# Merging two accumulators at the end of an expert stage: VectorE adds and plain stores in place of GpSimd scatters

## The chip, the cores and the metric

The kernel runs on one core of one Trainium2 chip. The metric is the device time of one execution in microseconds (us); the median of three runs stands for a kernel. A profile is one more execution, taken with the hardware profiler. It has its own time, and a span from its first to its last instruction.

## The reference, cut to what matters

A small vision-tower layer: a state-space kernel makes the tokens, a class token is added, then come attention and a mixture of 32 experts with the best 4 for each token, plus one shared expert. The end of it is what the change touches:

```python
probs = zeros((T, 32)).at[arange(T)[:, None], idx].set(topv)      # T = 2056 tokens, 4 experts each
for (wg, wu, wd, p) in experts:                                   # 32 of them
    acc = acc + p[:, None] * (silu(clip(x @ wg.T)) * clip(x @ wu.T)) @ wd.T
out = h + acc + shared_expert(x)                                  # (2056, 512) f32
```

## The kernel before, in words

Tokens are handled in 17 tiles of 128 rows by 512 columns of f32 (`NT = 17`; the last tile has 8 real rows, the rest of it is scratch). One tile is 256 KB, all 17 are 4.46 MB. The program runs four stages one after the other: `ssm_stage`, `attention_stage`, `route_stage`, `expert_stage`. Each is a block in which all engines run their own instruction streams and meet at its end.

`route_stage` leaves in DRAM the normalised tokens (`x_rows`), the output `acc` (named `out_dram` in the profile) holding the residual plus the shared expert (stores at L968), and a second accumulator `acc2` (`acc_rows` in the profile) filled with zeros (17 stores from a zero tile, L960).

`expert_stage` goes over slots. A slot is up to 128 tokens of one expert; there are 96 slots in 24 passes of four (`UN = 4`), and a pass whose slots are all empty is skipped by a value that each engine reads (`used`, L1401). In this input 21 passes are used and the last three are skipped. In a slot GpSimd gathers the rows (L1562), TensorE transposes them and multiplies with the expert's weights (L1468, L1505), which SP loads (L1419), ScalarE scales the result into `ys` (L1527), and GpSimd scatters `ys` into an accumulator with an add done by the DMA (L1594): even slots into `acc`, odd slots into `acc2`. So two neighbouring slots never add into the same tensor at once. SP waits for each scatter to land (L1441) and passes that on by `landed` and `sent`.

After the passes comes the merge, which is what the change rewrites:

- SP leaves its loop over the passes, then reads the number of used passes four times (`turns`, L1405) and waits each time for the last weight loads (L1444), and only then issues 17 loads of 256 KB from `acc2` into the SBUF tile `back` (L1448).
- GpSimd waits until the first six tiles of `back` are in (then the next six, then the last five, `PARTS`) and issues 17 indirect scatters, one for a tile, that add `back` into `acc` by row numbers held in `rowids` (L1617). `rowids` is a small table loaded by SP at the start of the stage (L1412), between the load of `ident` (L1411) and the first weights (L1416 to L1419).
- GpSimd waits until all 17 have landed. The program ends there.

TensorE, VectorE and ScalarE have no work in the merge.

Of the kernel before, what the change touches and what calls it, by code (L numbers as in the profile page):

```python
# [11 lines left out]
DM = 512  # L12
# [5 lines left out]
NT = 17  # L18
# [5 lines left out]
UN = 4  # L24
# [1319 lines left out]
def expert_stage(nc, T, slot_info, slot_rows):  # L1344
# [6 lines left out]
    f32, i32 = mybir.dt.float32, mybir.dt.uint32  # L1351
    ALU, ACT = mybir.AluOpType, mybir.ActivationFunctionType
# [6 lines left out]
    with ExitStack() as ctx:  # L1359
        sb = lambda name, shape, dt=f32: ctx.enter_context(nc.sbuf_tensor("ex_" + name, shape, dt))  # L1360
        sem = lambda name: ctx.enter_context(nc.semaphore("ex_" + name))
        rowids = sb("rowids", [128, NT], i32)
        back = sb("back", [128, NT, DM])
        rowids_ready, added, landed = sem("rowids_ready"), sem("added"), sem("landed")
        PARTS = [range(0, 6), range(6, 12), range(12, NT)]
        rows_back = [sem(f"rows_back{k}") for k in range(len(PARTS))]
        ident = sb("ident", [128, 128])
        wt = sb("wt", [128, WBUF * WCOLS])
        gidx = [sb(f"gidx{n}", [128, 1], i32) for n in range(4)]
# [24 lines left out]
        pe_turn, pool_turn, sp_turn = (sem(n) for n in ("pe_turn", "pool_turn", "sp_turn"))  # L1394
# [4 lines left out]
        def used(engine, it):  # L1399

            return engine.If(engine.value_load(slot_info[0:1, bass.ds(it * (4 * UN) + 3, 1)], min_val=0, max_val=1))  # L1401

        def turns(engine):

            return engine.value_load(slot_info[0:1, 4 * 127 + 3:4 * 128], min_val=1, max_val=ITERS)  # L1405

        with nc.Block() as block:

            @block.sync
            def _(sp):  # L1410
                sp.dma_start(ident[:], T["ident"]).then_inc(ident_ready, 16)  # L1411
                sp.dma_start(rowids[:], T["rowids"]).then_inc(rowids_ready, 16)  # L1412

                def load(slot, n):

                    expert = sp.value_load(slot_info[0:1, bass.ds(slot * 4, 1)], min_val=0, max_val=NEXP - 1)  # L1416
                    first = sp.value_load(slot_info[0:1, bass.ds(slot * 4 + 1, 1)], min_val=0, max_val=1)
                    buf = sp.value_load(slot_info[0:1, bass.ds(slot * 4 + 2, 1)], min_val=0, max_val=WBUF - 1)
                    sp.dma_start(wt[:, bass.ds(buf * WCOLS, WCOLS)],  # L1419
                                 T["wexp"][bass.ds(expert, 1), :, :].rearrange("o p n -> p (o n)"),  # L1420
                                 cond=first).then_inc(w_ready[n % UN], 16)

                for slot in range(AHEAD):
                    if slot >= UN:
                        sp.wait_ge(w_ready[slot % UN], 16)
                        sp.sem_inc(sp_turn, 1)
                    load(slot, slot)
                sp.sem_inc(y_full, W_SEED)
                sp.sem_inc(landed, 2)
                with sp.Fori(0, ITERS) as it:  # L1430
                    with used(sp, it):
                        for n in range(UN):

                            sp.wait_ge(y_full, it * UN + n - 2 + W_SEED)
                            sp.sem_inc(sp_turn, 1)
                            sp.wait_ge(w_ready[(n + AHEAD) % UN], (it + (n + AHEAD) // UN - 1) * 16 + 16)
                            sp.sem_inc(sp_turn, 1)
                            load(it * UN + n + AHEAD, n + AHEAD)

                            sp.wait_ge(scattered[n % 2], (it * (UN // 2) + n // 2) * 16 + 16)  # L1440
                            sp.sem_inc(landed, 1)  # L1441
                            sp.sem_inc(sent, 1)
                for n in range(UN):
                    sp.wait_ge(w_ready[n], turns(sp) * 16 + (32 if n < AHEAD - UN else 16))  # L1444
                    sp.sem_inc(sp_turn, 1)
                for k, part in enumerate(PARTS):
                    for t in part:
                        sp.dma_start(back[:, t, :], T["acc2"][128 * t:128 * t + 128, :]).then_inc(rows_back[k], 16)  # L1448

            @block.tensor  # L1450
            def _(pe):
# [58 lines left out]
            @block.scalar  # L1510
            def _(act):
                A = nc.scalar
                act.sem_inc(ta_taken, TA_SEED)
                act.sem_inc(y_ready, Y_SEED)
                act.sem_inc(sent, SENT_SEED)
                with act.Fori(0, ITERS) as it:
                    with used(act, it):
                        for n in range(UN):
                            s = it * UN + n
                            act.wait_ge(gate_ready, s + 1)  # L1520
                            A.activation(sil[:], gc[:], ACT.Silu).then_inc(silu_ready, 1)  # L1521
                            act.wait_ge(ta_full, s + 1)
                            A.copy(actT[:].rearrange("p c t -> p (c t)"), ta[:, 0:FF]).then_inc(ta_taken, 1)
                            act.wait_ge(y_full, s + 1 + W_SEED)
                            act.wait_ge(sent, s + 1)
                            act.wait_ge(share_ready, s + 1)
                            A.activation(ys[n][:], yb[n % 2][:], ACT.Copy, scale=share[:, n:n + 1]).then_inc(y_ready, 1)  # L1527

            @block.vector
            def _(dve):  # L1530
                V = nc.vector

                def take_rows(n, count):
                    dve.wait_ge(tx_full, count)
                    V.tensor_copy(xT[n % 2][:].rearrange("p k t -> p (k t)"), tx[:]).then_inc(tx_taken, 1)  # L1535

                dve.sem_inc(tx_taken, TX_SEED)
                dve.sem_inc(gu_taken, GU_SEED)
                take_rows(0, 1)
                take_rows(1, 2)  # L1540
                with dve.Fori(0, ITERS) as it:  # L1541
                    with used(dve, it):
                        for n in range(UN):
                            s = it * UN + n
                            dve.wait_ge(gu_full, s + 1)
                            V.tensor_scalar(gc[:], gu[n % 2][:, 0:FF], -ALPHA, ALPHA, ALU.max, ALU.min).then_inc(gate_ready, 1)  # L1546
                            V.tensor_scalar(uc[:], gu[n % 2][:, FF:2 * FF], -ALPHA, ALPHA, ALU.max, ALU.min).then_inc(gu_taken, 1)  # L1547
                            dve.wait_ge(gu_taken, s + 2)
                            dve.wait_ge(silu_ready, s + 1)
                            V.tensor_tensor(act_[:], sil[:], uc[:], ALU.mult).then_inc(act_ready, 1)  # L1550
                            take_rows(n + 2, s + 3)

            @block.gpsimd
            def _(pool):
                P = nc.gpsimd
# [29 lines left out]
                with pool.Fori(0, ITERS) as it:  # L1585
                    with used(pool, it):
                        for n in range(UN):
# [8 lines left out]
                                                 None, compute_op=ALU.add).then_inc(scattered[n % 2], 16)  # L1596
# [9 lines left out]
                last = turns(pool)  # L1606
                for n in range(4):

                    pool.wait_ge(gathered[n], last * 16 + (32 if n < 2 else 16))
                    pool.sem_inc(pool_turn, 1)  # L1610
                pool.wait_ge(landed, last * UN + 2)
                pool.sem_inc(pool_turn, 1)
                pool.wait_ge(rowids_ready, 16)
                for k, part in enumerate(PARTS):
                    pool.wait_ge(rows_back[k], 16 * len(part))
                    for t in part:
                        P.indirect_dma_start(T["acc"], bass.IndirectOffsetOnAxis(ap=rowids[:, t:t + 1], axis=0), back[:, t, :],  # L1617
                                             None, compute_op=ALU.add).then_inc(added, 16)
                pool.wait_ge(added, 16 * NT)


def build(nc, T):
# [16 lines left out]
def laid_out(x, cls_tok, L0_tok_log_dt, L0_tok_B_ri, L0_tok_inv_A_real, L0_tok_A_imag, L0_attn_c_attn_w, L0_attn_c_attn_b,  # L1639
# [9 lines left out]
    k, v = slice(DM, DM + HD), slice(DM + HD, DM + 2 * HD)  # L1649
    selh = np.zeros((128, 4, 128), np.float32)  # L1650
    for j in range(4):
# [6 lines left out]
    row, col = np.arange(128)[:, None], np.arange(128)[None, :]  # L1658
# [14 lines left out]
        "upper": (row < col).astype(np.float32),  # L1673
        "iota": np.broadcast_to(col, (128, 128)).astype(np.float32),
        "rowid": row.astype(np.float32),
        "rowids": (row + 128 * np.arange(NT)[None, :]).astype(np.uint32),
        "isrow": (row < NCH).astype(np.float32),
        "router": chunks(L0_ffn_router_w.T),
        "ebias": L0_ffn_expert_bias.reshape(1, NEXP),
# [18 lines left out]
```

## Time and profile before

| | |
|---|---|
| median of 3 runs | 1371.49 us (1370.15 to 1372.88) |
| time of the profiled execution | 1373.46 us |
| its span | 1371.7 us |
| granted TensorE clock, mean | 0.916 of full speed |
| TensorE busy | 1059.8 us (77%) |
| VectorE, ScalarE, GpSimd busy | 633.5, 360.5, 427.0 us |
| moved by DMA | 138.05 MB |

The span is 1.76 us shorter than the profiled execution's own time, and that time is 1.97 us over the median of the runs. Differences worked out in the span are therefore applied to the median. A busy share is an average over four stages with different limits; the merge is the last 50 us or so and is read by itself. In the profile a name such as SPq or POOLq is an engine's sequencer: instructions that issue, read a register or wait. The DMA share of a stretch is the mean busy share of the core's 16 DMA engines, and it can read slightly over 1.

### The profile page before, as it was taken

How to read it: one execution, taken by the hardware profiler on the slowest of the kernel's cores; microseconds unless marked ns; L12 is line 12 of the kernel's file. 1: busy time of each engine (PE TensorE's matmuls, PEld its weight loads, DVE VectorE, ACT ScalarE, POOL GpSimd, SP SyncE). 2: the span in 40 equal slices, each digit the busy share in tenths (PEclk: the TensorE clock that was granted, in tenths of full speed). 3: DMA queues.
4: the chain of work that ended last, by engine and by line, in shares of the span. 5: the costliest groups of instructions: out<-in, count | busy, mean ns of one | idle time of the engine just before them, and what ended most of it. 6: DMA issues, size and time to landing. Idle time of an engine off the chain costs nothing. (4 is left out here: it accounts for less than half of the span.)

```text
span 1371.7 us, 23002 instructions
## 1 busy us (share of the span) xinstructions
PE 1059.8 (77%) x5647; PEld 648.9 (47%) x5649; DVE 633.5 (46%) x1459; ACT 360.5 (26%) x1030; POOL 427.0 (31%) x602
## 2 busy tenths in 40 slices
PE   0444368888868888859898399999999999999910
PEld 0343367677657777734344144444444444444400
DVE  8999744543426544563986523233232332323300
ACT  2111035454425554513100012222222222222200
POOL 0000032122012221110007634545545455454535
PEclk9766779999979999979999699999999999999965
DMA  4144400000000000041051348666687877656868
GB/s 151 25 69 77 77 1 2 1 1 2 1 3 1 1 1 1 2 141 60 1 193 46 105 103 227 134 183 175 182 227 178 254 197 195 169 132 168 240 170 130
DMA packets 58684, 138.05 MB, mean 101 GB/s; under 512 B 22624, under 2 KB 23648, under 8 KB 53872
## 3 DMA queue, kind: packets, MB, share of 16 engines
q0 software_dynamic: 21744, 51.56, 20.1%
q1 hardware_dynamic: 36864, 85.55, 18.6%
q8 instruction: 39, 0.64, 0.2%
q14 instruction: 37, 0.30, 0.1%
HBM read 180.81 MB, written 44.35 MB: 164 GB/s over the span
## 5 line engine op out<-in xcount | busy, mean ns | idle before, releaser
L1468 PE MATMUL ex_gu<-ex_wt,ex_xT 128*128 x680 | 324.7, 600 | 16.3 <-DVE ex_uc L1547 9.2
L1468 PEld LDWEIGHTS ex_gu<-ex_wt,ex_xT 128*128 128x128 f32 x680 | 121.9, 192 | 146.9 <-issue 146.9
L1535 DVE COPY ex_xT<-ex_tx 128x512 f32<-128x512 f32 x86 | 59.5, 691 | 252.0 <-PE ex_tx L1459 252.0
L1505 PE MATMUL ex_y<-ex_wt,ex_actT 128*128 x336 | 158.1, 593 | 0.0
L1527 ACT ACTIVATE ex_ys<-ex_y,ex_share 128x512 f32<-128x512 f32 x84 | 57.7, 687 | 294.3 <-PE ex_y L1505 287.3
L639 ACT ACTIVATE at_pg<-at_S,at_nmax 128x129 f32<-128x129 f32 (+1 forms) x256 | 104.9, 423 | 72.0 <-DVE at_nmax L751 65.3
L751 DVE TENSOR_REDUCE at_nmax<-at_S 128x1 f32<-128x129 f32 (+1 forms) x256 | 81.9, 353 | 78.2 <-PE at_S L519 72.6
L1562 POOL DMA_INDIRECT ex_xg<-x_rows,ex_gidx x90 | 90.3, 1004 | 73.4 <-POOL ex_gidx L1559 71.3
L1594 POOL DMA_INDIRECT out_dram<-ex_ys,ex_sidx x42 | 67.1, 1597 | 97.0 <-ACT ex_ys L1527 96.2
L329 PE MATMUL ssm_ps<-ssm_v,ssm_q 64*64 64x64 f32 x1024 | 46.6, 273 | 63.5 <-DVEq L287 63.5
L1594 POOL DMA_INDIRECT acc_rows<-ex_ys,ex_sidx x42 | 66.9, 1593 | 82.8 <-ACT ex_ys L1527 77.1
L1550 DVE TENSOR_TENSOR ex_act<-ex_sil,ex_uc 128x256 f32<-128x256 f32 x84 | 35.8, 426 | 115.5 <-ACT ex_sil L1521 115.5
L817 POOL TENSOR_TENSOR at_rstd<-at_ve,at_power 128x2 f32<-128x2 f32 x8 | 5.7, 712 | 245.2 <-DVE at_ve L687 245.2
L1340 POOL TENSOR_SCALAR rt_rowsel<-rt_iota,rt_posf 128x128 bf16<-128x128 f32 x68 | 45.6, 689 | 106.1 <-DVE rt_posf L1279 99.1
L329 PEld LDWEIGHTS ssm_ps<-ssm_v,ssm_q 64*64 64x64 f32 x1024 | 45.5, 183 | 65.3 <-DVEq L287 65.3
L1505 PEld LDWEIGHTS ex_y<-ex_wt,ex_actT 128*128 128x128 f32 x336 | 57.3, 190 | 40.2 <-issue 40.2
L1023 PE MATMUL rt_p<-rt_xT,rt_sgu 128*128 128x512 f32 (+1 forms) x160 | 64.9, 571 | 5.1 <-DVE rt_uc L1163 4.6
L1459 PEld LDWEIGHTS ex_tx<-ex_ident,ex_xg 128*128 128x128 f32 x344 | 43.2, 142 | 53.8 <-issue 53.8
L1567 POOL COPY ex_share<-ex_xg 128x1 f32 x86 | 65.8, 765 | 1.4 <-DMA ex_xg<-x_rows,ex_gidx 1.4
L1570 POOL COPY ex_sidx<-slot_rows 128x1 uint32 (+1 forms) x85 | 64.8, 762 | 0.0
L1459 PE MATMUL ex_tx<-ex_ident,ex_xg 128*128 128x128 f32 x344 | 52.1, 274 | 8.4 <-DMA ex_xg<-x_rows,ex_gidx 8.4
L519 PE MATMUL at_S<-at_maskb,at_identb 128*128 128x128 bf16 x256 | 57.7, 225 | 0.0
(305 smaller groups left out, 2020.9 us busy)
## 6 DMA issues: line engine op xcount, KB each, us to landing
ex_wt<-in_wexp_dram SPq DMA_DIRECT2D x89, 1536.0 KB
acc_rows<-rt_zero SPq DMA_DIRECT2D x17, 256.0 KB, 5.2
x_rows<-rt_xa SPq DMA_DIRECT2D x16, 272.0 KB
ex_back<-acc_rows SPq DMA_DIRECT2D x17, 256.0 KB, 5.7
ssm_rows<-ssm_c SPq DMA_DIRECT2D x8, 512.0 KB, 3.8
H<-ssm_rows SPq DMA_DIRECT2D x16, 256.0 KB, 5.6
out_dram<-H SPq DMA_DIRECT2D x16, 256.0 KB
at_watt<-in_watt_dram SPq DMA_DIRECT2D x1, 1536.0 KB, 8.5
```

The lines of the kernel that those rows point to most:

```text
L329: last = nc.tensor.matmul(ps[n][h, i, :], qb[n][h, r, i].rearrange("q c a -> q (c a)"), vb[n][h, r, i, :], start=(r == 0), stop=(r == 1))
L639: A.activation(pg[:, g % 2, m, 0:keys], S[m][:, 0:keys], ACT.Exp, bias=nmax[:, m:m + 1], accum_out=r2[:, n % 2, 4 * j + m:4 * j + m + 1]). ...
L751: V.tensor_reduce(out=nmax[:, m:m + 1], in_=S[m][:, 0:keys], axis=AX.X, op=ALU.max, negate=True).then_inc(max_done, 1)
L1023: last = M(gu[m][:, 0:n], sgu[:, kc, 128 * m:128 * m + 128], xT[:, kc, 128 * tiles[0]:128 * tiles[0] + n], start=(kc == 0), stop=(kc == KC ...
L1459: last = nc.tensor.transpose(tx[:, 128 * kc:128 * kc + 128], xg[n % 4][:, 128 * kc:128 * kc + 128], ident[:])
L1468: last = M(gu[n % 2][:], xT[n % 2][:, kc, :], wt[:, bass.ds(base + kc * 2 * FF, 2 * FF)], start=(kc == 0), stop=(kc == KC - 1))
L1505: last = M(yb[n % 2][:], actT[:, c, :], wt[:, bass.ds(base + KC * 2 * FF + c * DM, DM)], start=(c == 0), stop=(c == FC - 1))
L1535: V.tensor_copy(xT[n % 2][:].rearrange("p k t -> p (k t)"), tx[:]).then_inc(tx_taken, 1)
L1562: P.indirect_dma_start(xg[n % 4][:], None, T["x2"], bass.IndirectOffsetOnAxis(ap=gidx[n % 4][:], axis=0)).then_inc(gathered[n % 4], 16)
L1567: P.tensor_copy(share[:, n % 4:n % 4 + 1], xg[n % 4][:, bass.ds(expert + DM, 1)]).then_inc(share_ready, 1)
L1570: P.tensor_copy(sidx[n % UN][:], slot_rows[:, bass.ds(slot, 1)]).then_inc(sidx_ready, 1)
L1594: P.indirect_dma_start(T["acc2"] if n % 2 else T["acc"], bass.IndirectOffsetOnAxis(ap=sidx[n][:], axis=0), ys[n][:], None, compute_op=ALU. ...
```

## The change

Both accumulators are loaded into SBUF: `acc2` into `odd` by SP, `acc` into `even` by ScalarE's queue. Each is loaded in five parts of 4, 4, 4, 3 and 2 tiles, one DMA for a part. VectorE adds a part as soon as both of its halves are in, and SP stores it to `acc`. `rowids`, its load and the 17 scatters are gone. The waits for the last weight loads with their reads of `turns` now come after the stores have been issued, and SP waits for the stores at the end. ScalarE starts its loads when SP signals that it has left its loop (`all_landed`).

```diff
--- before.py
+++ after.py
@@ -1359,11 +1359,11 @@
     with ExitStack() as ctx:
         sb = lambda name, shape, dt=f32: ctx.enter_context(nc.sbuf_tensor("ex_" + name, shape, dt))
         sem = lambda name: ctx.enter_context(nc.semaphore("ex_" + name))
-        rowids = sb("rowids", [128, NT], i32)
-        back = sb("back", [128, NT, DM])
-        rowids_ready, added, landed = sem("rowids_ready"), sem("added"), sem("landed")
-        PARTS = [range(0, 6), range(6, 12), range(12, NT)]
-        rows_back = [sem(f"rows_back{k}") for k in range(len(PARTS))]
+        odd, even = sb("odd", [128, NT, DM]), sb("even", [128, NT, DM])
+        landed, all_landed, summed, stored = sem("landed"), sem("all_landed"), sem("summed"), sem("stored")
+        PARTS = [range(0, 4), range(4, 8), range(8, 12), range(12, 15), range(15, NT)]
+        odd_back = [sem(f"odd_back{k}") for k in range(len(PARTS))]
+        even_back = [sem(f"even_back{k}") for k in range(len(PARTS))]
         ident = sb("ident", [128, 128])
         wt = sb("wt", [128, WBUF * WCOLS])
         gidx = [sb(f"gidx{n}", [128, 1], i32) for n in range(4)]
@@ -1409,7 +1409,6 @@
             @block.sync
             def _(sp):
                 sp.dma_start(ident[:], T["ident"]).then_inc(ident_ready, 16)
-                sp.dma_start(rowids[:], T["rowids"]).then_inc(rowids_ready, 16)
 
                 def load(slot, n):
 
@@ -1440,12 +1439,18 @@
                             sp.wait_ge(scattered[n % 2], (it * (UN // 2) + n // 2) * 16 + 16)
                             sp.sem_inc(landed, 1)
                             sp.sem_inc(sent, 1)
+                sp.sem_inc(all_landed, 1)
+                for k, part in enumerate(PARTS):
+                    rows = T["acc2"][128 * part[0]:128 * part[-1] + 128, :].rearrange("(t p) d -> p t d", p=128)
+                    sp.dma_start(odd[:, part[0]:part[-1] + 1, :], rows).then_inc(odd_back[k], 16)
+                for k, part in enumerate(PARTS):
+                    rows = T["acc"][128 * part[0]:128 * part[-1] + 128, :].rearrange("(t p) d -> p t d", p=128)
+                    sp.wait_ge(summed, k + 1)
+                    sp.dma_start(rows, odd[:, part[0]:part[-1] + 1, :]).then_inc(stored, 16)
                 for n in range(UN):
                     sp.wait_ge(w_ready[n], turns(sp) * 16 + (32 if n < AHEAD - UN else 16))
                     sp.sem_inc(sp_turn, 1)
-                for k, part in enumerate(PARTS):
-                    for t in part:
-                        sp.dma_start(back[:, t, :], T["acc2"][128 * t:128 * t + 128, :]).then_inc(rows_back[k], 16)
+                sp.wait_ge(stored, 16 * len(PARTS))
 
             @block.tensor
             def _(pe):
@@ -1525,6 +1530,10 @@
                             act.wait_ge(sent, s + 1)
                             act.wait_ge(share_ready, s + 1)
                             A.activation(ys[n][:], yb[n % 2][:], ACT.Copy, scale=share[:, n:n + 1]).then_inc(y_ready, 1)
+                act.wait_ge(all_landed, 1)
+                for k, part in enumerate(PARTS):
+                    rows = T["acc"][128 * part[0]:128 * part[-1] + 128, :].rearrange("(t p) d -> p t d", p=128)
+                    act.dma_start(even[:, part[0]:part[-1] + 1, :], rows).then_inc(even_back[k], 16)
 
             @block.vector
             def _(dve):
@@ -1549,6 +1558,11 @@
                             dve.wait_ge(silu_ready, s + 1)
                             V.tensor_tensor(act_[:], sil[:], uc[:], ALU.mult).then_inc(act_ready, 1)
                             take_rows(n + 2, s + 3)
+                for k, part in enumerate(PARTS):
+                    tiles = slice(part[0], part[-1] + 1)
+                    dve.wait_ge(odd_back[k], 16)
+                    dve.wait_ge(even_back[k], 16)
+                    V.tensor_tensor(odd[:, tiles, :], odd[:, tiles, :], even[:, tiles, :], ALU.add).then_inc(summed, 1)
 
             @block.gpsimd
             def _(pool):
@@ -1608,15 +1622,6 @@
 
                     pool.wait_ge(gathered[n], last * 16 + (32 if n < 2 else 16))
                     pool.sem_inc(pool_turn, 1)
-                pool.wait_ge(landed, last * UN + 2)
-                pool.sem_inc(pool_turn, 1)
-                pool.wait_ge(rowids_ready, 16)
-                for k, part in enumerate(PARTS):
-                    pool.wait_ge(rows_back[k], 16 * len(part))
-                    for t in part:
-                        P.indirect_dma_start(T["acc"], bass.IndirectOffsetOnAxis(ap=rowids[:, t:t + 1], axis=0), back[:, t, :],
-                                             None, compute_op=ALU.add).then_inc(added, 16)
-                pool.wait_ge(added, 16 * NT)
 
 
 def build(nc, T):
@@ -1673,7 +1678,6 @@
         "upper": (row < col).astype(np.float32),
         "iota": np.broadcast_to(col, (128, 128)).astype(np.float32),
         "rowid": row.astype(np.float32),
-        "rowids": (row + 128 * np.arange(NT)[None, :]).astype(np.uint32),
         "isrow": (row < NCH).astype(np.float32),
         "router": chunks(L0_ffn_router_w.T),
         "ebias": L0_ffn_expert_bias.reshape(1, NEXP),
```

## Rows read from the trace of the kernel before

**Rows 1.** Chain of waits, expert stage only: shares by line.

```profile
by line: PE ex_gu L1468 57.6%; PE ex_y L1505 21.1%; PE ex_tx L1459 7.2%; PE ex_ta L1497 5.7%; issue 3.4%; DVEq L1401 2.2%; DVE ex_uc L1547 1.6%; DVEq L1541 0.6%; DVE ex_gc L1546 0.4%; DVE ex_xT L1535 0.3%; DVEq L1545 0.2%
```

**Rows 2.** Chain of waits, last slot to first scatter of the merge: start, length, what.

```profile
1309.30 0.69 ACT ex_ys L1527
...
1310.80 4.69 DMA acc_rows<-ex_ys,ex_sidx
...
1315.60 0.06 issue
...
1319.70 0.27 SPq L1405
...
1322.56 0.35 SPq L1448
...
1324.85 4.72 DMA ex_back<-acc_rows
...
1330.39 1.60 POOL out_dram L1617
```

**Rows 3.** Chain of waits, its last piece.

```profile
1360.18 1.55 POOL out_dram L1617
```

**Rows 4.** Busy time by stretch: five engines' busy us, TensorE's clock, DMA share, GB/s.

```profile
1322.56:1323.60 1.04, 0.00 (x0) 0.00 (x0) 0.00 (x0) 0.00 (x0) 0.00 (x0) 0.50 0.09 14
1324.00:1330.00 6.00, 0.00 (x0) 0.00 (x0) 0.00 (x0) 0.00 (x0) 0.00 (x0) 0.50 0.93 319
1326.00:1327.00 1.00, 0.00 (x0) 0.00 (x0) 0.00 (x0) 0.00 (x0) 0.00 (x0) 0.50 0.72 260
1340.00:1360.00 20.00, 0.00 (x0) 0.00 (x0) 0.00 (x0) 0.00 (x0) 16.82 (x11) 0.50 1.06 154
1364.00:1365.00 1.00, 0.00 (x0) 0.00 (x0) 0.00 (x0) 0.00 (x0) 0.00 (x0) 0.50 0.74 129
1365.00:1366.00 1.00, 0.00 (x0) 0.00 (x0) 0.00 (x0) 0.00 (x0) 0.00 (x0) 0.50 0.11 18
```

**Rows 5.** DMA queues, 1322 to 1372 us: packets, MB, share of 16 engines' time.

```profile
q0 software_dynamic: 2448, 4.46, 59.4%
q1 hardware_dynamic: 2448, 4.46, 25.9%
```

**Rows 6.** Start of the expert stage, chain of waits.

```profile
775.32 0.42 SPq L1412
...
775.77 0.51 SPq L1416
...
778.12 7.89 DMA ex_wt<-in_wexp_dram
...
787.11 6.59 PE ex_gu L1468 x8
```

**Rows 7.** Busy time by stretch, three others with the DMA engines full.

```profile
610.00:622.00 12.00, 10.36 (x44) 6.34 (x45) 11.52 (x30) 4.87 (x9) 3.17 (x2) 0.77 1.05 404
5.00:12.00 7.00, 0.00 (x0) 0.00 (x0) 6.45 (x20) 0.00 (x0) 0.00 (x0) 1.00 1.01 417
708.00:712.00 4.00, 3.85 (x9) 1.62 (x10) 3.86 (x6) 0.00 (x0) 0.00 (x0) 1.00 1.01 374
```

**Rows 8.** SP's DMA issues by line: ns min/median/max, first and last start.

```profile
L960 SPq DMA_DIRECT2D acc_rows<-rt_zero x17: 432/655/1411, 605.3 to 618.2; - x17
L137 SPq DMA_DIRECT2D ssm_rows<-ssm_c x8: 376/377/393, 61.9 to 161.4; - x8
```

**Rows 9.** VectorE groups by form: count, busy us, mean ns, idle.

```profile
L244 DVE TENSOR_TENSOR ssm_products<-ssm_c,ssm_work 128x2048 f32<-128x2048 f32 x2 | 4.5, 2284 | 0.0
L246 DVE TENSOR_TENSOR ssm_q_low<-ssm_products 128x1024 f32<-128x1024 f32 x1 | 1.2, 1224 | 0.0
```

**Rows 10.** Line L1617, issue to landing of its 17 scatters.

```profile
DMA to landing us min/median/max: 4.9/5.6/8.0
```

**Rows 11.** Busy time by stretch, one load of 16 partitions (L133).

```profile
68.00:69.00 1.00, 0.00 (x0) 0.00 (x0) 1.00 (x2) 0.00 (x0) 0.00 (x0) 0.50 1.06 107
```

## Prediction, on record before the changed kernel was run

> **What bounds the kernel now.** I began with the chain of waits over the expert stage. Four TensorE lines hold 91.6% of it [rows 1], so until 1309.30 the kernel goes at TensorE's pace, and nothing that VectorE, ScalarE or GpSimd do in the passes matters. Then I read the chain through the end [rows 2]. The last scatter of the passes is issued at 1310.80 and lands 4.69 us later. SP then walks through three skipped passes, and by 1319.70 it has left its loop. From 1319.70 to 1322.56 it only reads `turns` four times. Then it issues the loads of `acc2`. The first six tiles are in at 1329.57, GpSimd begins at 1330.39, and its last scatter is issued from 1360.18 for 1.55 us [rows 3]. The 17 scatters take (1361.73 - 1330.39) / 17 = 1.84 us each.
>
> The view of busy time by stretch says what else is full there. Between 1340 and 1360 GpSimd is busy for 16.82 of 20 us, but the DMA engines show a share of 1.06 while they move only 154 GB/s [rows 4]. So the merge is bound twice: by GpSimd's issue and by adding transfers that occupy the DMA engines far longer than plain ones. The view of the queues puts a price on that. 17 plain loads and 17 adding scatters move the same 4.46 MB, the loads for 25.9% and the scatters for 59.4% of the 16 engines' 50 us [rows 5]. That is 12.95 us against 29.7 us. TensorE, VectorE and ScalarE are idle there. DMA activity ends at about 1365.15 (share 0.74 in 1364 to 1365, 0.11 in the next us [rows 4]); to the end of the span at 1371.7 there are 6.55 us of landing and of the program's end.
>
> From SP's first load at 1322.56 to the end of DMA activity the merge so takes 42.6 us.
>
> **The change part by part.**
>
> The four reads of `turns` move behind the stores. SP can issue its first load where the reads begin now: 1322.56 - 1319.70 = 2.86 us sooner [rows 2], less about 0.05 us for the new signal to ScalarE. Gain **2.8 us**. The moved reads and their waits for weights, long landed, stand behind the last store's issue on SP. Nobody waits for them but SP's own last wait, and the stores in flight cover them; without that cover they would cost their 2.86 us again.
>
> The load of `rowids` goes. SP issues it from 775.32, and the weights' first instruction follows at 775.77; the weights set when the first multiplication starts [rows 6]. So everything behind moves by **0.45 us**. The chain from there on is TensorE's [rows 1], and I take the gain as kept; the other end is 0.
>
> The issue of the new DMAs. Ten large ones take the place of 17 loads on SP; each holds 512 pieces of 2 KB (384 or 256 in the last two). SP issues a DMA of 2,048 pieces in 0.38 us, no more than one of 128 pieces [rows 2, 8], so issue isn't a term. ScalarE's issue isn't in this trace; by the nearest row it is 0.4 us, and as both queues feed the same full engines, even 1 us there would be hidden behind the `odd` part that SP has already issued. Where the engines can't keep up, the issuing sequencer is held: for the 17 zero stores the median is 0.655 us, 256 KB / 0.655 us = 400 GB/s, the transfer's pace [rows 8]. SP will be held so in its loads, and the stores issued after them start later; but ScalarE and SP have nothing else to do, and the engines are full meanwhile.
>
> The traffic is the big term. 2 x 4.46 MB are loaded and 4.46 MB stored. Loads: the nearest row is the present load of `acc2`, the same tensor, rows and direction. It took 12.95 us of all engines [rows 5], or 344 GB/s; twice that is 25.9 us. The ends: the 319 GB/s of its undisturbed stretch [rows 4] gives 8.92 MB / 319 = 27.9 us, the 417 GB/s of the program's first loads [rows 7] gives 21.4 us. I take 25.9. Stores: the zero stores have the same form and ran at 404 GB/s [rows 7], 11.0 us; the slower end is the 374 GB/s of the stores at 708 to 712 us, 11.9 us. Together 36.9 us. Engines take 1.04 us after the first issue to begin, with a share of 0.09 until then [rows 4]: I use 1.1 us. From the first issue to the end of activity the new merge takes 38.0 us in place of 42.6. Gain **4.6 us**.
>
> A rule speaks for more. The Trainium skill, page "DMA: Bandwidth & Descriptors", section "Bandwidth", asks for transfers of 1 MiB and more, and its table has 425 GB/s for 16 MB against 138 for 64 KB. By that the loads would take 21.0 us, and the whole gain would be 4.9 us larger. The rows don't bear it out as a rule of size: the zero stores reached 404 GB/s with 256 KB each [rows 7, 8].
>
> VectorE's additions. A part of four tiles is 128x2048, 2.28 us [rows 9]; two tiles 1.22; three about 1.75 between them: 3 x 2.28 + 1.75 + 1.22 = 9.8 us. They lie under 36.9 us of traffic. The last counts only if the engines run dry before its store arrives. Behind the last load there are about 1.5 us of landing (estimate from the 1.04 us of start), the 1.22 us addition, 0.43 us of issue and 1.1 us of start: 4.2 us. Covering it are the stores of the parts before, 15 tiles or 3.93 MB, 9.7 us at 404 GB/s, if they are still due then. I take 0; uncovered it is 4.2 us.
>
> The end. GpSimd's scatters land 4.9 to 8.0 us after issue, median 5.6 [rows 10], so most of the 6.55 us is the program's end, which stays. I take no change; 1 us less, as GpSimd then reaches its end early, or 1.5 us more are the ends.
>
> The sum: 2.8 + 0.45 + 4.6 = **7.85 us**. The profiled span is 1371.7 us (its execution 1373.46, 1.97 over the median of 1371.49); the difference goes on the median: 1371.49 - 7.85 = **1363.6 us**.
>
> **The rivals.**
>
> *The loads run as fast as the engines can.* 417 GB/s for the loads saves 4.5 us more, and 1 us goes at the end: 1358.1 us. For it: two queues and larger DMAs keep more pieces waiting at every engine, and the share fell to 0.72 in one microsecond of the present load [rows 4]. Against it: that load was issued faster (256 KB in 0.47 us) than it moved, so a lack of issued work wasn't its limit.
>
> *The engines run dry before the last store.* If stores pass in among the loads, little is left when the last load lands, and 4.2 us show: 1367.8 us. For it: stores and loads share the engines, and the first part is summed long before the last has landed. Against it: SP's stores are issued behind all of its loads, and SP is held in those.
>
> *The rows of a part are read in an order that the memory or the engines serve badly, and it gets slower.* Now each DMA moves 256 KB that lie together. The new ones take for each partition four rows that lie 256 KB apart. This has one place, the 13.37 MB of the merge, and one price. The gains leave 42.6 - 1.1 + 2.8 + 0.45 = 44.75 us for them, so it is slower than now below 13.37 MB / 44.75 = 299 GB/s, and by over 0.2% below 281. At the 260 GB/s of the present load's worst microsecond [rows 4] it takes 51.4 us: 1371.49 + 6.7 = 1378.2 us. The far row is the load of `H`, whose rows too go several to a partition, with 107 GB/s at a share of 1.06 [rows 11]: 125 us, some 1452 us. But that one fills 16 partitions, the new ones 128 like the present loads. A rule stands beside it: the same page of the Trainium skill, section "Latency and other measured facts", has copies falling to 207 GB/s when the rows of neighbouring partitions lie 512 KiB apart. By it the merge would take 65 us and the kernel about 1392. Here neighbouring partitions lie 2 KB apart and only the four rows of one partition are far apart, and no run so far shows such a load.
>
> **How the numbers follow.** This kernel's runs lie within 0.2% of each other, 2.7 us, so less than that can't be told from no change. The forecast case has a chance of 0.54, its own range 1360 to 1368.5 (loads at 319, stores at 374 GB/s and a longer end give 39.8 us of traffic and 3.0 us of gain). Fast loads have 0.20, the dry engines 0.12, the badly served rows 0.14. For 8 in 10 I go from 1357 to 1370: it holds nearly all of the first three. Faster by over 0.2% (under 1368.8): 0.53 + 0.20 + 0.09 = 0.82. Slower (over 1374.2): 0.10 of the badly served rows. The same: what is left, 0.08.
>
> **What would show it.** SP's first load at about 1319.3, the chain's first multiplication 0.45 us sooner. Over the merge a DMA share near 1 and 340 to 400 GB/s without a gap. DMA activity ending near 1357, and 6.5 us after it. Five additions of 2.28, 1.75 and 1.22 us, the first at about 1327. The prediction is wrong if the loads' rate lies under 300 GB/s, if a stretch of low share stands between the last load and the last store, or if the end grows by several us.

## The result, and the profile after

Timed on one chip with the kernel before, the changed kernel took 1355.12 us (median of 4, 1354.44 to 1357.51) against 1372.18. The ratio is 0.9879, 95% interval 0.9861 to 0.9898: 17.1 us faster, between 14.0 and 19.1. Forecast were 1363.6 us and a range from 1357 to 1370; the direction was right, the gain was about twice the forecast, and the time lies below the range. Timed again later, the same kernel took 1354.69 us.

The profiled execution took 1354.81 us, its span is 1352.8. First the chain of waits at the end of the passes, to be read against [rows 2]:

```profile
1305.14 0.69 ACT ex_ys L1532
...
1306.64 4.44 DMA acc_rows<-ex_ys,ex_sidx
...
1311.69 0.26 SPq L1401
...
1312.99 0.27 SPq L1401
...
1314.26 0.26 SPq L1401
...
1315.29 0.51 ACTq L1536
1315.83 0.55 ACTq L1536
...
1321.33 20.90 DMA ex_even<-out_dram
...
1342.33 1.22 DVE ex_odd L1565
```

From the last `ys` to the first load there are 10.15 us, where before there were 13.26 (1309.30 to 1322.56): the reads of `turns` are out of the way. What stays in front is the landing of the last scatter and three skipped passes of 1.28 us each (L1401, from one start to the next).

The view of busy time by stretch over the merge (five engines, TensorE's clock, DMA share, GB/s), against [rows 4]:

```profile
1316.00:1318.00 2.00, 0.00 (x0) 0.00 (x0) 0.00 (x0) 0.00 (x0) 0.00 (x0) 0.50 0.61 102
1318.00:1323.00 5.00, 0.00 (x0) 0.00 (x0) 0.00 (x0) 0.00 (x0) 0.00 (x0) 0.50 0.97 347
1323.00:1342.00 19.00, 0.00 (x0) 0.00 (x0) 8.64 (x4) 0.00 (x0) 0.00 (x0) 0.50 1.04 391
1342.00:1351.00 9.00, 0.00 (x0) 0.00 (x0) 1.22 (x1) 0.00 (x0) 0.00 (x0) 0.50 1.05 409
1351.00:1352.00 1.00, 0.00 (x0) 0.00 (x0) 0.00 (x0) 0.00 (x0) 0.00 (x0) 0.50 0.86 332
```

The engines are full from 1318 to the end of activity at about 1351.9. The first microseconds are slow (347 GB/s), as they were before (319), then come 391 and 409. From the first load to the end of activity there are 36.6 us in place of 42.5. The additions lie under the traffic: the one of two tiles ends at 1343.55, and the engines are busy for 8 us after it.

Then the instructions of line L1407, where the stage's block ends, which the prediction left out. Each row has the engine, the kind, its ns and its start; a drain is the instruction with which an engine closes its part of the block. First the kernel before, then the changed one.

```profile
L1407 POOLq COMPARE_BRANCH  x1: 46/46/46, 1365.9 to 1365.9; - x1
L1407 POOLq DRAIN  x1: 5369/5369/5369, 1366.1 to 1366.1; - x1
```

```profile
L1407 POOLq DRAIN  x1: 3985/3985/3985, 1313.8 to 1313.8; - x1
...
L1407 DVEq DRAIN  x1: 1236/1236/1236, 1342.4 to 1342.4; - x1
L1407 SPq COMPARE_BRANCH  x1: 38/38/38, 1352.4 to 1352.4; - x1
L1407 SPq DRAIN  x1: 13/13/13, 1352.6 to 1352.6; - x1
```

In this stage GpSimd ends with a drain of 4 to 5.4 us. Before, it began at 1366.1, when the last scatter had landed, and ended at 1371.5: it was the end of the program. Now it runs from 1313.8 to 1317.8 beside the loads, and SP, which waits for the stores, drains in 0.013 us. From the end of DMA activity to the end of the span there are 0.9 us in place of 6.6. GpSimd's drain isn't long everywhere. This is the one at the end of the attention stage (L467), in which GpSimd computes but issues no DMA, from the trace of the kernel before:

```profile
L467 POOLq DRAIN  x1: 53/53/53, 555.4 to 555.4; - x1
```

What makes it 0.05 us there and 4 us in the expert stage no run separates; GpSimd's gathers and scatters are one difference between the two.

So the 18.9 us between the two spans are: 4.2 us up to the last `ys`, 3.1 from there to the first load, 5.9 in the traffic, 5.7 at the end.

### The profile page after: what moved, and what is told of

It reads as the page before. It is cut to its first block and busy times, and to the rows that moved or that the text cites. A ratio compares the mean times of both kernels' runs of the same rounds, so it can differ in the third digit from the quotient of the medians.

```text
span 1352.8 us, 22990 instructions
## 1 busy us (share of the span) xinstructions
PE 1057.3 (78%) x5647; PEld 648.3 (48%) x5649; DVE 643.6 (48%) x1464; ACT 360.6 (27%) x1030; POOL 400.9 (30%) x585
## 5 line engine op out<-in xcount | busy, mean ns | idle before, releaser
L1023 PE MATMUL rt_p<-rt_xT,rt_sgu 128*128 128x512 f32 (+1 forms) x160 | 62.1, 550 | 5.1 <-DVE rt_uc L1163 4.6
```

Source lines behind the costliest of these rows:

```text
L1023: last = M(gu[m][:, 0:n], sgu[:, kc, 128 * m:128 * m + 128], xT[:, kc, 128 * tiles[0]:128 * tiles[0] + n], start=(kc == 0), stop=(kc == KC ...
```

## The experiments

Each is read by stage: last `ys` to first load, first load to the end of DMA activity ("traffic"), and that to the end of the span ("end"). The changed kernel has 10.15, 36.6 and 0.9 us; timed again, 10.5, 36.2 and 1.2. The end of activity is read from stretches of 0.25 us, so traffic and end are good to a few tenths of a us. The time up to the last `ys` differs by some microseconds between executions of one program and isn't read from single ones; only in the part on the table it is compared, counted from the start of the stage.

**Whose wait it is.** In the kernel before, SP waits for the scatters in place of GpSimd.

```diff
+                sp.wait_ge(added, 16 * NT)     # SP, after its loads
-                pool.wait_ge(added, 16 * NT)
```

> The kernel before, with one edit: SP, not GpSimd, waits for the 17 scatters to land, so that GpSimd reaches the end of its block right after issuing them. Theory (the drain of GpSimd at the end of the block is a fixed cost that began only after its wait): the drain of about 5.4 us now begins about 4.3 us sooner, beside the landing of the last scatter, so from the end of DMA activity to the end of the span there are 1.5 to 2.5 us in place of 6.55, and the time falls by 4 to 5 us. Rival (adding scatters are reported late, whoever waits for them): the stretch stays at 6 to 6.6 us and the time stays.

1370.67 us against 1372.75 in one execution each; the end is 4.8 us in place of 6.6.

```profile
1359.40 1.55 POOL L1618 DMA_INDIRECT out_dram<-ex_back,ex_rowids  x1 [0.30 <-issue]
```

```profile
L1407 POOLq DRAIN  x1: 29963/29963/29963, 1338.7 to 1338.7; - x1
L1407 SPq COMPARE_BRANCH  x1: 38/38/38, 1365.1 to 1365.1; - x1
L1407 SPq DRAIN  x1: 13/13/13, 1365.3 to 1365.3; - x1
```

SP passes its wait at 1365.1, so the scatters have landed by then. GpSimd's drain stands in its queue from 1338.7, while its scatters are still being issued, the last from 1359.40 for 1.55 us; it ends at 1368.7 (1338.7 + 29.96). That is 3.6 us after the landing. So both expectations missed: the end shrank, by 1.8 us and not by 4 to 5. Freed of the wait, GpSimd still ends the program, and its drain is still running 5.4 us after its last scatter was issued (1360.95).

**GpSimd waits too.** In the changed kernel, GpSimd also waits for the last store.

```diff
+                pool.wait_ge(stored, 16 * len(PARTS))     # GpSimd's last instruction
```

> The changed kernel, with one edit: GpSimd also waits for the last store before it ends. Theory (GpSimd's drain is hidden only because GpSimd ends early): the span's stretch after the last DMA activity grows from 0.9 us to about 5, by the 4.0 us that the drain takes in the changed kernel. Rival (the 6.55 us belonged to the scatters): it stays at about 1 us.

1358.13 us in one execution; traffic 36.2, end 5.2 us.

```profile
L1407 POOLq COMPARE_BRANCH  x1: 43/43/43, 1351.7 to 1351.7; - x1
L1407 POOLq DRAIN  x1: 3987/3987/3987, 1351.9 to 1351.9; - x1
L1407 SPq DRAIN  x1: 13/13/13, 1351.9 to 1351.9; - x1
```

Here no adding scatter is near, everything has landed, and the drain still takes 3.99 us after GpSimd's last wait. With one wait the 4 us are back: the end is 4.3 us longer than in the changed kernel, 4.0 longer than in its repeat. So the drain behind GpSimd's wait is the cause of about 4 of the 5.7 us at the end. The other 1.4, by which the drain of the kernel before was longer (5.37 against 3.99), no run explains.

**GpSimd stores.** In the changed kernel, the five stores are issued by GpSimd; SP waits for them.

```diff
-                    sp.wait_ge(summed, k + 1)
-                    sp.dma_start(rows, odd[:, part[0]:part[-1] + 1, :]).then_inc(stored, 16)
+                    pool.wait_ge(summed, k + 1)     # the loop moves to GpSimd's end
+                    P.dma_start(rows, odd[:, part[0]:part[-1] + 1, :]).then_inc(stored, 16)
```

> The changed kernel, with the five plain stores issued by GpSimd instead of SP; SP still waits for them and GpSimd only issues. The last store lands some 9 us after its issue, since the stores before it are queued. Theory (GpSimd's drain can't be done before what GpSimd has issued has landed, and takes 3.6 to 5.4 us after that): from the end of DMA activity to the end of the span there are 4.5 to 6.5 us. Rival (the drain is a fixed piece of 4 to 8 us after GpSimd's last instruction): it is over when the last store lands, and the stretch stays at 1 to 1.5 us.

1357.07 us in one execution; traffic 36.6, end 4.2 us, which is outside both expectations. The premise was wrong: on GpSimd's queue the stores pass in among the loads, so that the last one landed 3.2 us after its issue and not 9, and the last loads came later instead.

```profile
1346.97 1.22 DVE L1561 TENSOR_TENSOR ex_odd<-ex_odd,ex_even 128x1024 f32<-128x1024 f32 x1 [1.73 <-DMA ex_even<-out_dram]
1348.49 0.71 POOL L1624 DMA_DIRECT2D out_dram<-ex_odd  x1 [2.21 <-DVE ex_odd L1561]
```

The view of that store alone, and then line L1407:

```profile
DMA to landing us min/median/max: 3.2/3.2/3.2
```

```profile
L1407 POOLq DRAIN  x1: 6233/6233/6233, 1348.5 to 1348.5; - x1
L1407 SPq COMPARE_BRANCH  x1: 38/38/38, 1351.7 to 1351.7; - x1
```

The drain ends at 1354.7, 3.0 us after SP sees the landing, and again it is the end of the program. In the kernel before and these three it ended 3.0 to 5.6 us after the last landing. That it waits for what GpSimd issued fits the first and third experiments, but as no transfer here landed long after its issue, it isn't separated from a drain that simply ends 5.5 to 7.8 us after the last issue.

**The reads of `turns` in front again.** In the changed kernel they move from behind the stores to their old place:

```diff
+                for n in range(UN):
+                    sp.wait_ge(w_ready[n], turns(sp) * 16 + (32 if n < AHEAD - UN else 16))
+                    sp.sem_inc(sp_turn, 1)
                 sp.sem_inc(all_landed, 1)
```

> The changed kernel, with the reads of the number of passes and their waits for weights back in front of the loads. Theory: SP's first load of the merge issues 2.8 to 2.9 us later after the last scatter's landing, and the whole merge behind it is unchanged, so plus 2.8 us. Rival (the reads were hidden, since ScalarE or the engines weren't ready before): less than 1 us.

Last `ys` to first load: 13.16 us, 3.0 more; traffic 36.3, end 1.1; 1358.56 us in one execution. The term stands.

```profile
1305.89 0.70 ACT ex_ys L1532
...
1316.16 0.27 SPq L1405
...
1319.05 0.50 ACTq L1536
```

**One queue; small loads; rows together.** Three edits of the traffic in the changed kernel: all loads on SP; 17 loads of 256 KB on each queue; and the rows dealt to the partitions in another way.

```diff
-                    act.dma_start(even[:, part[0]:part[-1] + 1, :], rows).then_inc(even_back[k], 16)
+                    sp.dma_start(even[:, part[0]:part[-1] + 1, :], rows).then_inc(even_back[k], 16)     # first edit
...
+                    for t in part:                                                                      # second edit
+                        sp.dma_start(odd[:, t, :], T["acc2"][128 * t:128 * t + 128, :]).then_inc(odd_back[k], 16)
...
-  .rearrange("(t p) d -> p t d", p=128)
+  .rearrange("(p t) d -> p t d", p=128)                                # third edit, loads and stores
```

> The changed kernel, with both accumulators loaded by SP, part by part in turn, and none by ScalarE. Theory (the 16 engines were full either way, and my 344 GB/s was low because the profile's share of the old loads counts time in which adding scatters shared the engines): the merge from SP's first load to the end of DMA activity stays at 36.5 us, within 1 us, with about 385 GB/s once it has started. Rival (two queues are what keeps the engines full): about 340 to 350 GB/s for the loads, 39 to 40 us.

> The changed kernel, with 17 loads of 256 KB on each of the two queues in place of five large ones; the stores stay large. Theory (size doesn't matter once the engines are full): the merge stays at 36.5 us, within 1 us. Rival (large transfers are what brought the rate): the loads go at 320 to 350 GB/s, and the merge takes 38.5 to 40 us.

> The changed kernel, with the rows of a part dealt so that the four, three or two rows of a partition lie together in DRAM, 8 KB in one piece, for the loads and the stores alike; the sum is the same. Theory (rows 256 KB apart cost nothing here): the merge stays at 36 to 36.6 us. Rival (the far rows do cost): the rate rises from 390 towards the 417 GB/s of the program's first loads, which have pieces of 8 and 12 KB, and the merge takes 33 to 34.5 us.

Traffic: 36.3, 35.4 and 33.7 us; single executions of 1357.68, 1357.24 and 1355.30 us. The view of stretches, for one queue, then for small loads, then for rows together:

```profile
1320.00:1325.00 5.00, 0.00 (x0) 0.00 (x0) 0.00 (x0) 0.00 (x0) 0.00 (x0) 0.50 0.93 333
1325.00:1345.00 20.00, 0.00 (x0) 0.00 (x0) 9.16 (x5) 0.00 (x0) 0.00 (x0) 0.50 1.05 391
```

```profile
1320.00:1325.00 5.00, 0.00 (x0) 0.00 (x0) 0.00 (x0) 0.00 (x0) 0.00 (x0) 0.50 1.01 368
1325.00:1345.00 20.00, 0.00 (x0) 0.00 (x0) 8.84 (x5) 0.00 (x0) 0.00 (x0) 0.50 1.05 391
```

```profile
1324.00:1347.00 23.00, 0.00 (x0) 0.00 (x0) 9.86 (x5) 0.00 (x0) 0.00 (x0) 0.50 1.01 415
```

Neither the second queue nor the size of a transfer brought the rate: 391 GB/s each time once it runs, after a slower start. So the rivals of the first two are out, though the small loads fell just outside the 36.5 us within 1 that the theory gave them. For the third, the theory is out: rows that lie together, up to 8 KB in a piece, move at 415 GB/s, and the traffic takes 2.5 to 2.9 us less than with rows that lie 256 KB apart (36.2 and 36.6 us in two executions of the changed kernel). The small loads, which read 256 KB that lie together in pieces of 2 KB, gain 0.8 to 1.2 us; so how much of the gain is the distance and how much the piece isn't settled.

**The even accumulator earlier.** ScalarE doesn't wait for SP's signal but for the last scatter into `acc`.

```diff
-                act.wait_ge(all_landed, 1)
+                act.wait_ge(scattered[0], turns(act) * (16 * UN // 2))
```

> The changed kernel, with ScalarE itself waiting for the last scatter into the even accumulator, by the number of passes, instead of for SP's signal; SP still loads the odd one after its loop. Theory (the merge is bound by its traffic from the first load on, and SP's three skipped passes of 1.28 us each stand in front of it): ScalarE's first load issues 4.5 to 5 us sooner, the engines are busy from then on, and the time falls by 4 to 5 us against the changed kernel, to about 1350.5 us. Rival (SP's late odd loads set the end): less than 1.5 us.

1352.25 us, 0.9858 (0.9842 to 0.9875) of the kernel before, 2.9 us under the changed kernel's median of 1355.12 and short of the 4 to 5 expected. ScalarE's first load comes 3.80 us after the last `ys` in place of 10.15, but the traffic takes 38.1 us: until 1316 the engines move 252 GB/s, while the last scatter and the last gathers still run beside it.

```profile
1305.91 0.69 ACT L1531 ACTIVATE ex_ys<-ex_y,ex_share 128x512 f32<-128x512 f32 x1 [3.50 <-PE ex_y L1509]
...
1309.71 6.56 ACTq L1535 DMA_DIRECT2D ex_even<-out_dram  x5
```

```profile
1309.50:1316.00 6.50, 0.00 (x0) 0.00 (x0) 0.00 (x0) 0.00 (x0) 1.12 (x2) 0.50 0.97 252
```

From the last `ys` to the end of activity the profiled execution is 4.8 us shorter than the changed kernel's; of these 0.4 are lost at the end, and its last `ys` came 0.8 later, which the edit doesn't touch.

**The table of row numbers.** Its load is put back in the changed kernel, though nothing reads it (SP only waits for it at its very end); run once, then in rounds beside the changed kernel.

```diff
                 sp.dma_start(ident[:], T["ident"]).then_inc(ident_ready, 16)
+                sp.dma_start(rowids[:], T["rowids"]).then_inc(rowids_ready, 16)
```

> The changed kernel, with the load of the table of row numbers put back at its old place, though nothing reads it. Theory (only its issue was on the path): SP's first weight load issues 0.45 us later in its stage, and the first weights land about 6.5 us after issue as in the changed kernel; everything else as there. Rival (the table's 128 small pieces or the shifted addresses of all later tiles slow the first weights and the loads of the merge): the first weights take 7.5 to 8 us and the loads of the merge run below 350 GB/s.

> The changed kernel with the load of the table of row numbers put back, timed in rounds, since its single execution was 6 us over the changed kernel's median, most of it in the passes. Theory (the table costs its issue of 0.45 us and no more; the passes vary by some us between executions): the median is within 1.5 us of the changed kernel timed beside it. Rival (the shifted tiles or the small pieces slow the passes): 4 to 6 us above it.

> The changed kernel itself, timed again beside the others. Every theory: 1354 to 1357 us, 0.986 to 0.990 of the kernel before.

The single execution took 1360.93 us, the four in rounds 1357.07 (0.9889, 0.9874 to 0.9905); the changed kernel beside them 1354.69 (0.9876, 0.9858 to 0.9894). The merge is the same in both (traffic 36.4 and 36.5 us), so shifted tiles don't slow it. The medians are 2.4 us apart, more than the theory's 1.5 and less than the rival's 4; the intervals overlap. The single execution was no measure: 1.5 of its 6 us came before the stage began, and its first `ys` and its last lie 510.8 us apart, against 507.6 to 508.2 in the other three executions with the table. One place where the table could cost is the first weights, in the chain of waits of the table's execution in rounds:

```profile
775.88 7.85 DMA ex_wt<-in_wexp_dram
```

With the table they took 7.5 to 7.9 us in all four profiled executions that have it (the kernel before is one of them), without it 6.5 to 9.0 with a median of 6.65 in ten. So the rival of the single run was right about the first weights and wrong about the merge.

The last `ys` came between 1306.7 and 1311.0 in the four, between 1304.4 and 1308.1 in the ten. But the stage itself began at 772.7 to 777.1, by what happened before it. Counted from its first instruction, SP's load of `ident`, the passes can be compared in single executions. Here is that start in the kernel before, to be read with [rows 6]:

```profile
774.92 0.35 SPq L1411
```

And in the changed kernel:

```profile
773.97 0.36 SPq L1411
...
776.71 6.47 DMA ex_wt<-in_wexp_dram
...
784.28 5.18 PE ex_gu L1473 x8
```

The first multiplication starts 12.19 us into the stage before (774.92 to 787.11) and 10.31 after. From the start of the stage to the last `ys` there are 532.8 to 535.6 us in the four with the table (median 534.2; 534.1 without the single execution) and 530.7 to 533.7 in the ten without it (median 531.1). Only one of the ten is in the range of the four, the one whose first weights took 9.0 us. So by the traces the table was worth about 3 us. 0.45 of them are its issue, and about 1 the later landing of the first weights; where the rest lies no run shows.

**Both improvements.** The early wait and the rows together.

> ScalarE's own early wait together with the rows of a part dealt so that they lie together. Theory (the two gains are in different terms, the start of the traffic and its rate): from ScalarE's first load to the end of DMA activity 35 to 36 us in place of 38.1, and a time of 1349 to 1350.5 us, 0.983 to 0.985 of the kernel before. Rival (SP's odd loads come too late for the faster engines): no faster than with the early wait alone, 1352 us.

1347.01 us (1345.81 to 1348.52), 0.9816 (0.9802 to 0.9829) of the kernel before: 25 us faster than it and 7.7 under the changed kernel's median beside it. Traffic 36.2 us from a first load 3.78 us after the last `ys`.

```profile
1308.90:1315.00 6.10, 0.00 (x0) 0.00 (x0) 0.00 (x0) 0.00 (x0) 1.00 (x1) 0.50 0.89 264
1315.00:1340.00 25.00, 0.00 (x0) 0.00 (x0) 9.75 (x5) 0.00 (x0) 0.00 (x0) 0.50 1.01 417
```

Behind the mixed start the engines run at 417 GB/s. From the last `ys` to the end of the span the profiled executions took 47.7 us in the changed kernel and 48.0 in its repeat, 43.3 with the early wait, 45.5 with the rows together and 41.5 with both. So the gains nearly add up, as is to be expected when one starts the traffic sooner and the other raises its rate. The traffic missed its 35 to 36 us by a little, and the time came out below the expected 1349. Of the 7.7 us in the medians the merge has 6.2 to 6.5; the rest no run explains.

## Why the prediction was half right

*The reads of `turns`, 2.8 us.* Right: 3.0 to 3.1.

*The end, "I take no change".* This is the step that failed. I had read that a scatter lands 5.6 us after its issue and that 6.55 us follow the end of DMA activity, and had called the difference "the program's end, which stays". The end was an instruction of one engine, GpSimd's drain of 5.37 us, in the row of line L1407, and the change took GpSimd off the last wait. It measured 5.7 us gained, where I had allowed 1. The second experiment gives 4.0 to 4.3 of it back by one wait; why the drain of the kernel before was 1.4 us longer stays open.

*The traffic, 4.6 us.* The mechanism was right, the size was off: 5.9 us. I had taken 344 GB/s for the loads from 17 loads that took 12.95 us of engine time. That was a short burst, slow in its first 6 us (319), and later shared with adding scatters; which of the two made it low isn't separated. A stream three times as long runs at 391 to 409 after the same slow start. The rival of fast loads had the rate right in kind, but neither two queues nor larger transfers are its reason.

*Rows 256 KB apart.* The rival that ended slower had named a real cost, but one of 2.5 to 2.9 us; it would have needed 7.85 to undo the forecast gain. The rule that stood beside it (the Trainium skill, page "DMA: Bandwidth & Descriptors", section "Latency and other measured facts", 207 GB/s for rows of neighbouring partitions 512 KiB apart) has another case than this one; no run here shows it, and at 391 GB/s this kernel is far from that rate.

*Engines dry before the last store.* It didn't happen: SP's stores came behind its loads, and the engines were busy for 8 us after the last addition. The third experiment shows the other order, stores in among the loads, and there too the traffic took 36.6 us.

*`rowids`, 0.45 us.* The issue is gone as said, but the term was too small. I had left out that the first weights might land later behind the table. By the traces the stage up to the last `ys` is about 3 us shorter without it; the medians in rounds lie 2.4 us apart, with intervals that overlap.

By stages the reads of `turns`, the traffic and the end make 3.0 + 5.9 + 5.7 = 14.6 of the 17.1 us. The other 2.5 agree with the 2.4 to 3 us of the table, within the interval (14.0 to 19.1). Of the 4.2 us by which the two profiled executions differ up to the last `ys`, 1.0 came before the stage (774.92 against 773.97), which the change doesn't touch, and 3.2 within it.

## What to carry to other kernels

Ask of the last microseconds which engine runs the last instruction, and what it is: a drain that is hidden on an engine that ends early is paid in full on the one that waits last. Where a merge is bound by DMA traffic, sum the bytes by the rate of a long stream, not of a short burst, and look at when the first byte can move: here an engine that waited for its own half instead of for a signal was worth 2.9 us of the median, and dealing out the rows so that those of a partition lie together took 2.5 to 2.9 us off the traffic. And a small load in front of the first weights can cost more than its issue; compare such a term from the start of its stage, since what comes before a stage varies by itself.

## What the runs showed of the hardware that I had not expected

GpSimd's drain at the end of the expert stage took 3.99 us with everything landed, both when it began 3 us after its last gather was issued (changed kernel) and when it began 42 us after it, behind a wait (second experiment), against 0.013 us on SP and 0.15 us on ScalarE; at the end of the attention stage it took 0.05 us. The traffic took 36.3 us with all loads on one queue and 36.2 to 36.6 with two. Stores issued by GpSimd passed in among queued loads and landed after 3.2 us, those issued by SP behind its loads after 8.9 us, and the traffic as a whole took as long either way.
